# Banded attention and routed experts on one core: values block diagonal by their loads, blocks of 16 queries and 8 heads, tile lists for each 1024 tokens

## What is computed

```python
h = layernorm(x) * (1 + ca) + sa
# attention: 16 heads of 8 channels
scores = einsum('bhqd,bhkd->bhqk', q, k) / sqrt(8)
band   = abs(idx[:, None] - idx[None, :]) <= half        # half <= 60, from the data
attn   = softmax(where(band, scores, -1e30))
x = x + ga * ((attn @ v per head) @ W_o per head, joined) @ Wfc + bfc
h = layernorm(x) * (1 + cb) + sb
# router: 2 of 8 experts for each token
score = relu(h @ rw1 + rb1) @ rw2 + rb2;  gate = softmax(top 2 of score)
out   = sum over experts e of gate[:, e] * (relu(h @ W1[e] + b1[e]) @ W2[e] + b2[e])
return x + gb * out
```

## Time and profile before

| | us |
|---|---|
| median of 3 runs | 520.83 |
| lowest and highest run | 520.20, 522.73 |
| the profiled execution, its own time | 520.48 |
| its span, first to last instruction | 518.7 |
| PE / PE loads / DVE / ACT / POOL busy | 456.1 / 366.9 / 380.6 / 368.3 / 328.7 |
| mean granted TensorE clock | 0.956 of 2.4 GHz |

### The profile page before, as it was taken

How to read it: one execution, slowest core, us unless ns; L and a number is a source line. 1 busy time by engine, 2 the same in 40 slices (tenths; PEclk the granted TensorE clock), 3 DMA queues, 4 the chain that set the end, 5 groups by cost and what they waited for, 6 DMA issues and landing times.

```text
span 518.7 us, 17625 instructions
## 1 busy us (share of the span) xinstructions
PE 456.1 (88%) x5492; PEld 366.9 (71%) x5493; DVE 380.6 (73%) x998; ACT 368.3 (71%) x1545; POOL 328.7 (63%) x452
## 2 busy tenths in 40 slices
PE   6997999999999999999989993078999999999937
PEld 5565777776767777777654441068999999999937
DVE  6778999999999999999954674056454555578704
ACT  3677999999999999999966661034566665698720
POOL 5984655555556787877564377777777775545540
PEclk9999999999999999999999996568999999999977
DMA  8472111111111141141052022153343326323226
GB/s 202 128 223 80 43 46 37 36 38 43 44 44 42 47 142 34 44 121 35 3 181 35 12 77 64 51 118 79 94 109 100 90 85 210 91 72 102 81 81 197
DMA packets 64505, 43.58 MB, mean 84 GB/s; under 512 B 9246, under 2 KB 60230, under 8 KB 64298
## 3 DMA queue, kind: packets, MB, share of 16 engines
q1 hardware_dynamic: 58634, 33.02, 23.3%
q0 software_dynamic: 4544, 9.38, 5.3%
q10 hardware_dynamic: 1248, 0.20, 0.2%
HBM read 26.93 MB, written 15.64 MB: 82 GB/s over the span
## 4 chain that ended last, share of the span: by engine, by line
PE 44%; ACT 20%; DVE 17%; issue 9%; POOL 5%; DMA 2%; SPq 0%; DVEq 0%; ACTq 0%; POOLq 0%
ACT pr L1041 20%; PE pAm L1861 13%; DVE nmax L1107 8%; PE pSpm L1869 7%; PE pScm L1869 6%; PE pAm L1459 5%; POOL xs L1586 3%; DVE prT L1115 2%; PE pS L1069 2%; DVE oT L948 1%; PE pSpm L1466 1%; DMA x_all<-in_L_attn_x 1%; PE pO L903 1%; DVE stat L1339 1%; PE pScm L1474 1%
## 5 line engine op out<-in xcount | busy, mean ns | idle before, releaser
L1041 ACT ACTIVATE pr<-pS,nmax 128x152 f32<-128x152 f32 x512 | 192.0, 395 | 9.9 <-DVE nmax L1107 9.9
L1672 ACT ACTIVATE act<-pAm,w1t 128x128 f32<-128x128 f32 x312 | 89.8, 377 | 76.7 <-PE pAm L1861 76.3
L1041 ACT ACTIVATION_READ_ACCUMULATOR pr<-pS,nmax 128x1 f32 x512 | 109.5, 214 | 0.0
L1618 POOL DMA_INDIRECT y_scr<-ys,si x78 | 76.2, 977 | 44.8 <-PE pAm L1861 25.8
L1069 PE MATMUL pS<-kT,qbd 64*128 64x152 f32 x1024 | 100.6, 315 | 1.1 <-ACT pr L1041 0.8
L1107 DVE TENSOR_REDUCE nmax<-pS 128x4 f32<-128x608 f32 x128 | 96.3, 752 | 1.9 <-PE pS L1073 1.3
L1861 PE MATMUL pAm<-hgT,w1t 128*128 128x128 f32 x624 | 85.0, 281 | 2.1 <-DVE w1t L1728 2.1
L1115 DVE STREAM_TRANSPOSE prT<-pr 128x640 f32<-128x640 f32 x96 | 81.1, 845 | 4.5
L1069 PEld LDWEIGHTS pS<-kT,qbd 64*128 64x128 f32 x1024 | 71.7, 186 | 15.8 <-ACT pr L1041 1.1
L1861 PEld LDWEIGHTS pAm<-hgT,w1t 128*128 128x128 f32 x624 | 78.3, 197 | 2.4 <-DVE w1t L1728 2.2
L1586 POOL DMA_INDIRECT xs<-h_all,pos_i x64 | 63.4, 990 | 21.6 <-issue 17.4
(11 more groups left out here) (279 smaller groups left out, 694.5 us busy)
## 6 DMA issues: line engine op xcount, KB each, us to landing
vrep<-v_scr SPq DMA_DIRECT2D x132, 64.0 KB, 2.0
hg<-xs SPq DMA_DIRECT2D x78, 65.0 KB
h_all<-y_scr SPq DMA_DIRECT2D x16, 256.0 KB, 5.0
v_scr<-h_all SPq DMA_DIRECT2D x8, 256.0 KB, 2.7
out<-h_all SPq DMA_DIRECT2D x16, 128.0 KB
x_all<-in_L_attn_x SPq DMA_DIRECT2D x3, 512.0 KB, 7.1
w_all<-in_L_ffn_W SPq DMA_DIRECT2D x2, 768.0 KB, 4.7
w_all<-in_L_ffn_W SPq DMA_DIRECT2D x3, 512.0 KB, 6.1
```

What stands on the lines that cost most here:

```text
L1041: e.activation(pr[:, hg, q * WIN + EDGE:q * WIN + EDGE + SPAN], scored(j, gi)[:, lo:lo + SPAN], ACT.Exp, bias=nmax[:, k:k + 1], scale=-1.0 ...
L1618: e.indirect_dma_start(out=y_scr, out_offset=bass.IndirectOffsetOnAxis(ap=si[:, j:j + 1].bitcast(U32), axis=0), in_=ys[j % R // 2][:, j % ...
L1672: e.activation(ac(u)[:, k, :], pU[u % W][:, k, :], ACT.Relu, bias=w1t[u // 2 % 4][:, u % 2, FF + D + k:FF + D + k + 1]).then_inc(a_up.sem, 1)
```

## The change

In attention a score row's block becomes 16 queries and 8 heads (`QT`, `NH8`), so `SPAN` is 136; `pS` holds four such blocks as before, now of two groups of 8 heads and two groups of 16 queries. The values' products of `wv_sb` leave the four heads' channels interleaved, and four loads of 16 KB write them straight into the diagonal blocks of `vbd` (four sets, zeroed once at the start); `spread_values` and `vrep` are gone, and TensorE waits for the loads itself. `denominators` becomes a product on GpSimd, between the two halves of its queries; `spread` is two products of 64 x 128. `weighted` waits for three of the four transposes at first, and reads its stationary operand with a step of four elements.

The second norm is done on GpSimd alone, row by row and already modulated (`refined(g)` for 4 sets, `row_modulated`), so TensorE transposes `h_all` and VectorE has no rows to make in the router.

Lists of tiles are made for each 1024 tokens (`LISTS` = 0, 8, 24, 40, 72): the first three take full tiles only, the last takes what is left, `NF` = 72 (39 for each half before). List k waits for the dispatches of part k alone. The tile loop is written out (ring `ys` of 24 tiles), `in_step` is gone, each scatter of the last part stands behind two dispatches, and the first half is fetched after the last load and combined from tile 67 on.

```diff
+NH8 = H // 2
 QB = 32
+QT = 16
+QN = P // QT
 WIN = QB + 2 * HALO
 KW = P + 2 * HALO
...
-SPAN = WIN - 2 * EDGE
+SPAN = QT + 2 * (HALO - EDGE)
...
-SPARE = NE - 1
+SPARE = NE
 TH = T // 2
-NFH = TH * TOPK // FT + SPARE
-NF = 2 * NFH
-CAP = TH + FT
-HR = NE * CAP + SPARE * FT
+LISTS = (0, 8, 24, 40, 72)
+NL = len(LISTS) - 1
+NF = LISTS[-1]
+NB = LISTS[-1] - LISTS[-2]
+N0 = LISTS[-2] + NE
+CAP = T + FT
+ROWS = NE * CAP + SPARE * FT
 XR = D + 2
 ISQ = 1.0 / float(np.sqrt(HD))
 
...
-            def load_values(e, s, u):
+            def load_values(e, s):
 
                 for r in range(4):
-                    src = v_scr[bass.ds(s * P, P), :].rearrange("(n k) d -> k n d", k=QB)
-                    e.dma_start(vrep[u][QB * r:QB * r + QB, :, :], src).then_inc(d_v[u], 16)
-
-            def spread_queries(e, t, u):
-
-                for a in range(2):
-                    e.tensor_tensor(qbd[u][:, a, :, :].rearrange("p q (h t) -> p q h t", h=4),
-                                    qT[:, bass.ds(t * P, P)].rearrange("p (q a t) -> p q a t", q=4, a=1).broadcast_to([P, 4, 4, QB]),
-                                    strided(eqd[:, a, :], 0, [[0, 4], [1, 4], [0, QB]]), ALU.mult).then_inc(p_qb.sem, 1)
-
-            def spread_values(e, u):
-                return e.tensor_tensor(vbd[u][:, :, :].rearrange("p n (g h d) -> p (n g) h d", g=HG, h=4),
-                                       vrep[u][:, :, :].rearrange("p n (g h d) -> p (n g) h d", g=HG, h=4),
-                                       strided(eqh[:, :], 0, [[0, SB * HG], [1, 4], [0, HD]]), ALU.mult)
+                    src = v_scr[s * P:(s + 1) * P, QB * r:QB * r + QB].rearrange("(n k) d -> k n d", k=QB)
+                    e.dma_start(vbd[QB * r:QB * r + QB, s % VR, :, QB * r:QB * r + QB], src).then_inc(d_v[s % VR], 16)
+
+            def spread_queries(e, t, u, a):
+
+                e.tensor_tensor(qbd[u][:, 4 * a:4 * a + 4, :].rearrange("p q (h t) -> p q h t", h=NH8),
+                                qT[:, bass.ds(t * P + 4 * a * QT, 4 * QT)].rearrange("p (q a t) -> p q a t", q=4, a=1).broadcast_to([P, 4, NH8, QT]),
+                                strided(eqd[:, :], 0, [[0, 4], [1, NH8], [0, QT]]), ALU.mult).then_inc(p_qb.sem, 1)
 
...
                 e.memset(ident[:, :], 0.0).then_inc(p_con, 1)
+                e.memset(vbd[:, :, :, :].rearrange("p s n d -> p (s n d)"), 0.0).then_inc(p_vz, 1)
...
-                        mm = e.matmul(pV[:, n * P:(n + 1) * P], hT[j % 2][:, n * P:(n + 1) * P], wv_sb[:, :], start=True, stop=True)
+                        mm = e.matmul(pV[:, n * P:(n + 1) * P], hT[j % 2][:, n * P:(n + 1) * P], wv_sb[:, :].rearrange("p (g r d) -> p r d g", g=HG, r=4), start=True, stop=True)
...
                 if 0 in blocks:
+                    v_tr.wait(e, i, u, 3, back=1)
+                    if i == 0 and u == 1:
+                        e.wait_ge(d_v[0], 64)
+                    v_o.wait(e, i, u, back=1)
+                if 3 in blocks:
+                    e.wait_ge(d_v[(2 * i + u) % VR], 64 * ((2 * i + u) // VR + 1))
                     v_tr.wait(e, i, u, back=1)
-                    p_vb.wait(e, i, u)
-                    v_o.wait(e, i, u, back=1)
                 for n in blocks:
                     lo, hi = max(0, n - 4), min(3, n)
-                    values = vbd[(j - 1 + n // SB) % RING]
+                    values = vbd[:, (2 * i + u - 1 + n // SB) % VR, n % SB, :]
                     for hg in range(HG):
-                        mm = e.matmul(pO[32 * hg:32 * hg + 32, lo * QB:(hi + 1) * QB], values[:, n % SB, 32 * hg:32 * hg + 32],
-                                      strided(prT[w][:, hg, 0:1], n * QB + lo * (WIN - QB), [[WIN - QB, hi - lo + 1], [1, QB]]),
+                        mm = e.matmul(pO[32 * hg:32 * hg + 32, lo * QB:(hi + 1) * QB], strided(values, hg, [[HG, QB]]),
+                                      strided(prT[w][:, hg // 2, 0:1], 2 * WIN * lo + (n - lo) * QB + hg % 2 * QT,
+                                              [[2 * WIN - QB, hi - lo + 1], [WIN, 2], [1, QT]]),
                                       start=n == 0, stop=n == KBLK - 1, skip_group_check=True)
                 if KBLK - 1 in blocks:
                     mm.then_inc(t_o.sem, 1)
 
             def spread(e, i, u):
-                v_den.wait(e, i, u)
+                p_sp.wait(e, i, u)
                 a_r.wait(e, i, u, back=1)
                 a_x.wait(e, i, u, back=1)
-                for q in range(4):
...
-                e.transpose(rsT[:, :], rden[:, :]).then_inc(v_den.sem, 1)
+                e.tensor_tensor(rsp[:, :, :].rearrange("p n (q t) -> p (n q) t", t=QT), strided(rden[:, 0:1], 0, [[1, H], [0, QT]]),
+                                strided(eqt[:, 0:1], 0, [[0, H], [1, QT]]), ALU.mult).then_inc(p_sp.sem, 1)
...
+                for s in range(3, SETS):
+                    if s >= VR:
+                        t_o.wait(e, (s - VR + 1) // 2, (s - VR + 1) % 2)
+                    load_values(e, s)
+                    if s in LOADED:
+                        load_weights(e, *LOADED[s])
...
                 def turn(t):
                     if t + 2 < NT:
-                        queries((t + 2) // 2, t % 2, t + 2)
+                        queries((t + 2) // 2, t % 2, t + 2, 0)
+                    denominators(e, t // 2, t % 2)
+                    if t + 2 < NT:
+                        queries((t + 2) // 2, t % 2, t + 2, 1)
                     residual(e, t // 2, t % 2)
-                    if t + 2 <= NT:
-                        values((t + 2) // 2, t % 2, (t + 2) // 6, (t + 2) % 6)
...
+                    g, part = t // 4 - 2, t % 4
+                    if g >= 0:
+                        if part == 0:
+                            refined(e, g)
+                        for n in ((), (0,), (1, 2), (3,))[part]:
+                            row_modulated(e, 4 * g + n)
...
-            R = 16
+            R = 24
...
+            FROM = 65
+            RANKED = 9
+            LISTED = RANKED + 1
+            PAD_AT = LISTS[2] - 1
+            CHOSEN = 36
+            GATED = CHOSEN + 2
...
+            def row_modulated(e, n):
+                mine, b = h_all[:, n, 0:D], n // TPB
+                e.tensor_scalar(mine, x_all[:, n + 1, :], mv2[:, n, 0:1], rstd2[:, n:n + 1], ALU.subtract, ALU.mult).then_inc(p_mu, 1)
+                e.wait_ge(p_mu, 2 * n + 1)
+                e.tensor_tensor(mine, mine, cb_bc[:, b, :], ALU.mult).then_inc(p_mu, 1)
+                e.wait_ge(p_mu, 2 * n + 2)
+                e.tensor_tensor(mine, mine, sb_bc[:, b, :], ALU.add).then_inc(p_h2, 1)
...
+                def listed(k):
+
+                    e.wait_ge(v_fin, k + 1)
+                    e.wait_ge(d_x[k], 16 * 2 * (PARTS[k][1] - PARTS[k][0]))
...
+                    if j == PAD_AT:
+                        pads()
+                    if j == LISTS[-2]:
+                        e.wait_ge(d_pad, 16 * (1 + NE))
+                    if j in LISTS:
+                        listed(LISTS.index(j))
...
+                denominators(e, NI, 0)
+                refined(e, NG - 2)
+                residual(e, NI, 0)
+                for n in range(NT - 8, NT - 4):
+                    row_modulated(e, n)
...
+                sent = 0
                 for p, (first, end) in enumerate(PARTS):
                     routed(e, p)
                     for r in range(2 * first, 2 * end):
-                        in_step(m)
                         dispatch(e, r // 2, r % 2)
-                        m += 1
-                        if p == len(PARTS) - 1:
-                            in_step(m)
-                            scatter(r - 2 * first)
-                            m += 1
-                for j in range(2 * (end - first), NF):
-                    in_step(m)
+                        if p == len(PARTS) - 1 and r % 2 == 1:
+                            scatter(sent)
+                            sent += 1
+                for j in range(sent, NF):
                     scatter(j)
```

574 lines of the change are left out of this document (263 added, 311 removed).

## The result

The change takes **573.0 us** (median of 4 runs, 570.4 to 573.9) against 521.1 (4 runs, 520.2 to 522.7): a ratio of **1.099**, 95% interval 1.094 to 1.103. The profiled execution is the one of 570.43 us, its span 568.5, its mean granted clock 0.885 instead of 0.956. Forecast were 496 us, with a range of 485 to 511. The prediction is wrong in sign and size.

The account below looks back on a forecast made before the run. VectorE was taken as nearest to attention's bound, TensorE as binding the tile loop. Attention -11.2, start +0.5, attention to last tile -19.1 and tail +4.9 gave -24.9 against 520.48: 496 us, range 485 to 511.

Parts of the forecast that it names:

- Attention: 32 attention steps: each falls from 6.78 to 6.43 us, 11.2 us less in all, with ends of 15 and 3.
- GpSimd binds attention: Rival in attention: inverse sums take 1.04 us, steps 6.78 us from step 8 on; +8 us, 504 us; 15%.
- The sign that the prediction set for itself: Attention: a step over 6.6 us would mean GpSimd or the loads, told by who releases TensorE and VectorE.
- The size of one product: Attention: inverse sums on GpSimd 0.61 us, VectorE's reductions near 690 ns, a step 6.43 us.
- TensorE's weight loads: Weighted sums in attention: strided loads stay at 109 ns each.
- f: Factor by which strided weight loads lengthen: 1 expected, hidden up to 1.6; 7% for 1.6 to 2.3, 10% above.
- Start: Before attention: the memset of the values' buffer delays TensorE's first matmuls, +0.5 us (0 to +2).
- Attention to the last product: From attention to the last tile's product: 19.1 us less, 11.2 of it from six tiles less.
- First hole: TensorE's idle time before the first expert tile shrinks from 24 us to 5.
- second: New hole inside the tile loop, at the transposes of tile 8, waiting for gathered rows: 10 to 13 us.
- Tail: Last product to the end: second half's first fetch moves from 5.7 to 10.6 us after it, +4.9 us (0 to 7).
- The slower rival: TensorE's strided weight loads bind attention; f over 2.3 makes the kernel slower, f = 3 gives 548 us; 10%.

Follow-up runs that it names:

- e6: The change with GpSimd's turn reordered as in e5 and its 26 refinement and row operations dealt over four turns: 570.8 us where before takes 551.9; attention 204.94 us.
- e12: The change with e6's queue and values' weights copied into order once (566.6 us), plus weighted sums' weight loads reading neighbours, not every fourth element: 567.4 us.
- e17: The kernel before with its tile loop written out for TensorE, VectorE and ScalarE: 521.1 us, ratio 1.002.
- e19: The kernel of e17 measured again, on a chip where before takes 520.4: 522.2 us, ratio 1.003.
- e15: The change with GpSimd's queue of e6 and the values' weights copied into order once: 500.0 us, ratio 0.962.
- e5: The change with GpSimd's turn reordered: inverse sums, previous turn's residual, both query halves, then refinement or rows: 570.4 us where before takes 551.9; attention 206.95 us.

## Why the prediction was wrong, step by step

- **Attention, the step that failed.** The prediction said of GpSimd: "4 x (2.04 + 0.61 + 0.90) + 4.2 + 7.0 = 25.4 us against 4 x 6.43 = 25.7. It just fits. The heaviest turn (3.55 + 4.2) runs 1.3 us late; the inverse sums may be late by that". That is a sum of work against a time, and it holds: e6 with all of this work takes 6.61 us a step. What it left out is the order. GpSimd's wait for `xa` was in front of me as a row, 37.0 us in 15 residuals, and I let it count as room for the new work. Room it is only for what stands *ahead* of that wait. The change puts the work behind it and ahead of the inverse sums, and TensorE reads these in the same step. The slack on record was small: reciprocals 3.0 us ahead of the spreading; the values' product that GpSimd gave up was done 4.55 us before TensorE's step needed it (before: 149.64 and 154.19). So the whole of a turn's work (4.2, 1.85, 3.7, 1.85 us, 11.6 in four steps) was added to the step: 38.7 - 4 x 6.6 = 12.3 us in four steps. The other 0.7 us no run takes apart; the lower clock, which also lengthens the scores, is the likely reason. The rival "GpSimd binds attention" had the right engine and the wrong mechanism, and so a price of 8 us over the forecast instead of 60.7 + 10.9 = 72.

  The sign that the prediction set for itself, a step over 6.6 us and then who releases TensorE, points the right way: of the waits of TensorE between 60 and 325 us, 62.3 us end with `rsp` and 1.2 with `oT` of VectorE, none with the loads of `vbd`, whose wait was put at nothing.
- **The size of one product was right.** `rsp` was put at 0.61 us and took 0.617, the maxima at 690 ns and took 685 to 704. Without the ring a step was put at 6.43 us and took 6.60 in the change, 6.61 in e6. VectorE kept its 844 ns transposes, which with the maxima leave it full at 47.5 of 50.
- **TensorE's weight loads**: f = 1.33, hidden (e12). The forecast of 109 ns, f = 1, was wrong, its consequence right: up to f = 1.6 was to be hidden.
- **Start**: +0.5 forecast, +3.9 measured, read from a mark that scatters by 5 us (it stands at 43.7, 42.3 and 42.5 in before, e17 and e19). I counted the memset, which is there (TensorE's first wait is 3.4 us instead of 1.7), and overlooked the product with `wv_sb` in another order of columns, 7.1 us of TensorE's time, of which some 2 us show in the mark. The new order stands in the diff that the prediction had before it. The rest of the difference is open.
- **Attention to the last product**: -19.1 forecast, -19.3 measured. First hole 5 forecast, 3.58 + 0.8 in pieces measured; second 10 to 13 forecast, 9.95 measured (11.50 in e15); 17 products a tile, 1.87 us, 72 times.
- **Tail**: +4.9 forecast, +4.5 measured; the second half is first fetched 10.0 us behind the last product (10.6 forecast, 5.7 before); 27 us from the last product to the end forecast, 26.5 measured.
- **The slower rival** had 10% and a mechanism that did not decide. No case of the prediction had a wait that runs once around all engines, although every member of the ring stood in the rows.

## What to carry to other kernels

When work is moved to an engine with idle time, ask which event ends each idle stretch, and whether the work will stand ahead of that event or behind it in the engine's queue; idle time behind a late event is worth nothing. Write down, for each product on that engine, who waits for it and how many steps of slack it has, and put it in the queue by that: first what others need in this step, then what waits, then what has slack. In this kernel the order of one queue was worth 65 us of attention (272.1 in the change, 206.95 in e5), dealing out the refinement 2 us more, and the sum of busy times would have passed both orders.
